# A decoder layer on one core: pieces of TensorE's work parted at their inputs, and softmax sums taken from tiles that GpSimd has added

## What is computed

```python
x = x + self_attention(layernorm(x))              # 16 heads of 16, q and k rotated by position
x = x + cross_attention(layernorm(x), ctx_1024)   # 16 heads of 16, 77 keys
x = x + ffn(layernorm(x))

def ffn(inputs):                                  # six nodes, each an attention of 8 heads of 32
    nodes = {-1: inputs}
    for c in range(6):
        nsrc = min(c + 1, 5); snode = c - nsrc
        q = ew[c, 0] * (nodes[c - 1] @ We[lind + nsrc - 1] + be[...])
        k = ew[c, 1] * (nodes[snode] @ We[lind] + be[...])
        v = ew[c, 2] * (nodes[snode + nsrc // 2] @ We[lind + nsrc // 2] + be[...])
        nodes[c] = act_w[c] * mha(q, k, v, Wq[c], Wk[c], Wv[c], Wo[c]) + q
        lind += nsrc
    return layernorm(nodes[5], ln_g, ln_b)
```

## Time and profile before

| | |
|---|---|
| median of 3 runs | 5605.14 us |
| lowest and highest | 5601.58 and 5607.79 us |
| profiled execution | 5609.61 us, its span 5607.0 us |
| mean granted clock of TensorE | 0.945 of full speed |
| transfers | 46.66 MB, mean 8 GB/s |

### The profile page before, as it was taken

How to read it: one execution, slowest core, us unless ns; L and a number is a source line. 1 busy time by engine, 2 the same in 40 slices (tenths; PEclk the granted TensorE clock), 3 DMA queues, 4 the chain that set the end, 5 groups by cost and what they waited for, 6 DMA issues and landing times.

```text
span 5607.0 us, 154314 instructions
## 1 busy us (share of the span) xinstructions
PE 5142.0 (92%) x64216; PEld 3781.3 (67%) x64216; DVE 2855.0 (51%) x5090; ACT 2527.1 (45%) x4784; POOL 655.8 (12%) x1753
## 2 busy tenths in 40 slices
PE   5898999989999898998989999898998989989899
PEld 5576666767667676676767667676676766667676
DVE  2545554454554545455454554555445455554545
ACT  0354444444445354444444445444444444445444
POOL 0101001010110201001010110201002010110201
PEclk8899998999989899998999989899898999989999
DMA  3000000000000000000000000000000000000000
GB/s 120 6 2 10 3 2 11 2 11 2 7 5 2 11 2 10 3 2 11 2 11 2 6 7 2 11 2 10 3 2 11 2 10 3 6 7 2 11 2 7
DMA packets 45078, 46.66 MB, mean 8 GB/s; under 512 B 11968, under 2 KB 44096, under 8 KB 44352
## 3 DMA queue, kind: packets, MB, share of 16 engines
q1 hardware_dynamic: 36480, 28.59, 1.7%
q10 hardware_dynamic: 7872, 7.76, 0.4%
HBM read 27.95 MB, written 8.39 MB: 6 GB/s over the span
## 4 chain that ended last, share of the span: by engine, by line
issue 82%; POOL 9%; PE 2%; DVE 2%; POOLq 1%; DVEq 0%; ACT 0%; ACTq 0%
POOL neg_max L649 3%; POOL neg_max L652 2%; PE banks L856 2%; POOL x_tok L634 2%; POOL inv_std L628 1%; POOL rope_c L641 1%; DVE n_tok L788 0%; DVE rope_s L801 0%; POOL var_eps L625 0%; POOL node_t L659 0%; POOL node_t L656 0%; POOLq L648 0%; POOLq L651 0%; PE banks L915 0%; DVE rope_s L797 0%
## 5 line engine op out<-in xcount | busy, mean ns | idle before, releaser
L826 DVE TENSOR_REDUCE row_max<-banks 128x4 f32<-128x1024 f32 (+1 forms) x1288 | 1317.6, 1069 | 746.6 <-PE banks L856 711.3
L740 ACT ACTIVATE probs<-banks 128x1024 f32<-128x1024 f32 (+1 forms) x1288 | 1147.3, 936 | 608.0 <-PE banks L856 604.1
L856 PE MATMUL banks<-q_parts,k_parts 32*128 32x256 f32 x12384 | 591.6, 302 | 114.1 <-DVE row_max L826 69.4
L856 PEld LDWEIGHTS banks<-q_parts,k_parts 32*128 32x128 f32 x12384 | 464.3, 192 | 308.9 <-DVE row_max L826 187.4
L856 PE MATMUL banks<-k_parts,q_parts 32*128 32x256 f32 x12432 | 527.5, 302 | 148.2 <-DVE row_max L826 68.6
L837 DVE TENSOR_TENSOR probs<-banks,context_t 128x256 f32<-128x256 f32 x449 | 190.0, 423 | 903.2 <-ACT context_t L752 899.7
L856 PE MATMUL banks<-node_t,w_n 128*128 128x256 f32 x2560 | 641.7, 386 | 0.4
L856 PEld LDWEIGHTS banks<-k_parts,q_parts 32*128 32x128 f32 x12432 | 430.0, 193 | 298.9 <-issue 133.1
L649 POOL TENSOR_TENSOR neg_max<-row_max,zeros 128x8 fp32r<-128x8 f32 x644 | 141.5, 220 | 3749.5 <-DVE row_max L826 3749.5
L856 PEld LDWEIGHTS banks<-node_t,w_n 128*128 128x128 f32 x2560 | 461.9, 190 | 93.8 <-issue 26.3
L750 ACT ACTIVATE context_t<-banks 128x256 f32<-128x256 f32 x514 | 196.6, 383 | 611.6 <-PE banks L856 607.4
(11 more groups left out here) (126 smaller groups left out, 6485.0 us busy)
## 6 DMA issues: line engine op xcount, KB each, us to landing
x_next<-in_x SPq DMA_DIRECT2D x34, 256.0 KB, 2.6
out_y<-x_tok SPq DMA_DIRECT2D x32, 256.0 KB, 2.1
w_head<-in_wf SPq DMA_DIRECT2D x2, 1536.0 KB, 12.8
...
w_n<-in_we ACTq DMA_DIRECT2D x3, 256.0 KB, 11.5
```

The costliest lines, as they stand in the source:

```text
L740: done(act.activation(probs[s][0:rows, g % 2, 2 * p:2 * p + 2, 0:kt, :] .rearrange("p c k t -> p c (k t)"), psum[0:rows, b0:b0 + 2, 0:kt * T],
L826: done(dve.reduce_max(row_max[s][:, g, 2 * p:2 * p + 2, :].rearrange("p c q -> p (c q)"), psum[:, b0:b0 + 2, :].rearrange("p c (q t) -> p ...
L856: return nc.tensor.matmul(bank_ap, lhs, rhs, start=start, stop=stop, **kw)
```

## The change

- **Sums.** A new kind PA on GpSimd adds the probabilities of the two key tiles, one operation for two heads (p = 0 into `n_tok`, p = 1 into a new buffer `pair_sums`). PV keeps only the values; a new kind PS multiplies the added tiles by ones, 4 matmuls in place of 8. In cross attention PS takes the probabilities themselves. EX now waits for PV and PA of the buffer's last user, RC for PS, and LNN of stage 0 also for the last PS, since `n_tok` is shared.
- **Parted pieces.** Q becomes Q and QB (first and second half c of the input), each waiting for its half of the node; QH, QL and NE become one piece for each half d. S becomes S (high by high, high by low) and SB (low by high). ST becomes ST (the scores, waiting for the parts) and SX (the maxima, waiting for MR). OUT becomes OA (the query input) and two OB (one for each half of the context, each waiting for its NR).
- **Buffers.** `kx_parts` goes; cross attention keeps its keys in `k_parts`.
- **Order and banks.** `ORDER` is a new table with 942 words where it had 676. The loop's branch, before between S1.0.1 and S1.0.2, is now between K1.0 and OB0.0.1.

```diff
+            elif k == "PA":
+                g, p = a[3:]
+                both = probs[s][:, g % 2, 2 * p:2 * p + 2, :, :]
+                pool.wait_ge(sem["exp_done"], reached(at, "exp_done", ("EX", s, j, g, p)))
+                pool.wait_ge(sem["sums_ready"], reached(at, "sums_ready", old_sums(s, j, g)))
+                done(pool.tensor_tensor(added(s, p), both[:, :, 0, :], both[:, :, 1, :], ALU.add), "tiles_added", a)
...
+                old = old_probs(s, j, g)
+                act.wait_ge(sem["context_ready"], reached(at, "context_ready", ("PV",) + old))
+                if old[1] == CROSS:
+                    act.wait_ge(sem["sums_ready"], reached(at, "sums_ready", ("PS",) + old))
+                else:
+                    act.wait_ge(sem["tiles_added"], reached(at, "tiles_added", *[("PA",) + old + (i,) for i in range(2)]))
...
-                for what in range(2):
-                    for q in range(kt):
-                        for c in range(4):
-                            if what == 0:
-                                lhs = ones[0:m, :] if j >= FFN0 else half_ones[0:m, 16 * e:16 * e + 32]
...
+                for c in range(4):
+                    lhs = ones[0:m, :] if j >= FFN0 else half_ones[0:m, 16 * e:16 * e + 32]
+                    rhs = probs[s][0:m, g % 2, c, 0, :] if j == CROSS else added(s, c // 2)[:, c % 2, :]
+                    last = matmul(bank_of(a)[ROWS * c:ROWS * (c + 1), T:2 * T], lhs, rhs, False, True,
+                                  skip_group_check=True)
+                done(last, "sums_ready", a)
...
+                q_half = (s, j, 1 if j == SELF else x)
+                if k == "S":
+                    wait_for(pe, at, a, ("high_kept", ("QH",) + q_half), ("low_kept", ("KL", s, j)))
+                else:
+                    wait_for(pe, at, a, ("low_kept", ("QL",) + q_half))
...
-                wait_for(pe, at, a, ("max_rows_kept", ("MR", s, j, x)))
+                wait_for(pe, at, a, ("low_kept", ("QL", s, j, 1 if j == SELF else x)), ("low_kept", ("KL", s, j)))
...
+            elif k == "SX":
+                x, e = place(j, a[3])
+                wait_for(pe, at, a, ("max_rows_kept", ("MR", s, j, x)))
...
+                wait_for(pe, at, a, *(node_kept(s, j, "q") if k == "OA" else [("normalized", ("NR", s, j, a[3]))]))
```

Two lines of the new table, from stage 4:

```diff
+V0.4@5 VE0.4 S0.4.1@0 SB0.4.1 Q1.4@7 QB1.4 QH1.4.0 QH1.4.1 MT0.4.0@6 MR0.4.0 MX0.4.1.1 MX0.4.1.0 NM0.4.1
+ST0.4.0@0 SX0.4.0 EX0.4.0.1 PA0.4.0.1 EX0.4.0.0 PA0.4.0.0 QL1.4.0 QL1.4.1 S1.4.0@4 SB1.4.0 MX1.4.0.0 MX1.4.0.1
```

411 lines of the change are left out of this document (232 added, 179 removed).

## The result

| | before | after |
|---|---|---|
| median | 5605.07 us | 5755.25 us |
| lowest and highest | 5601.58 and 5607.79 us | 5752.68 and 5759.41 us |
| profiled execution | 5609.61 us | 5759.41 us, its span 5757.6 us |
| mean granted clock of TensorE | 0.945 | 0.929 |
| ratio to before | 1 | 1.0269, 95% interval 1.0251 to 1.0287 |

The account below looks back on a forecast made before the run. TensorE, busy 92% of the span, was taken as the bound. Terms of -14.1 + 2.4 + 2.9 + 1 + 1 + 0.6 gave -6.2 us a round, times 16, and -10 once: 5500 us from 5605, range 5400 to 5610.

Parts of the forecast that it names:

- The step that failed: Feed-forward stages: apart from the priced waits, parted pieces and adds were called well covered, so no cost was counted.
- The rival on GpSimd: Self-attention waits for GpSimd's adds at 1.72 us each: +1 us a round, 5611, with the clock below 5630; chance 0.14.
- The sums' matmuls: TensorE's matmuls with ones, 8 fewer in each of 32 groups: 14.1 us a round saved.
- The four waits of 1.2 us: Stages 3 to 6, TensorE waiting for slot 0's probabilities; net +2.4 us a round after old waits are covered.
- The step into stage 2: K0.3, TR1.2 and Q1.2 on TensorE wait for residual, layer norm and copy with less cover: +2.9 us a round.
- The head of slot 1: Branch leaves the maxima, but residual, layer norm, transpose and projection lack cover: +1 us a round, bounds -2 and +5.
- Self-attention of slot 0: GpSimd's eight adds and final scaling against some 16 us of TensorE pieces: +1 us a round, bounds 0 and +4.
- Changes of tile shape: TensorE's matmul shape changes go from 162 to 168 a round at 0.1 us each: +0.6 us a round.
- Ahead of the loop: Pieces before the loop's first scores no longer issued ahead: -10 us, once.
- The clock: Rival: new waits at stage 2 and slot 1's head keep the clock low, 3 us a round lost, 5548; chance 0.13.
- What was said of the profile after: Signs: ones at 3072 instructions, 64 adds a round, TensorE busy 220 us less, its waits 30 to 33 us a round.
- I am wrong if the round is over 336: Refutation sign; bracketed reasons: an add above 1.6 us in self-attention, or slot 1's head longer than taken.

Follow-up runs that it names:

- nm_first: The kernel after the change with three negated maxima moved ahead of the adds they stood behind in GpSimd's queue; 5565.0 us, 0.9926 of before.
- adds_first: The kernel after the change with two adds of slot 1, stage 6 moved ahead of a negated maximum in GpSimd's queue; 5696.8 us, 1.0161 of before.
- no_adds: The kernel after the change without GpSimd's adds: sums take both key tiles by 8 matmuls, parted pieces and order stay; 5600.3 us, 0.9992 of before.
- queue_all: The kernel after the change with the moves of nm_first and adds_first plus two places in self-attention, only GpSimd's order differing; 5481.9 us, 0.9775 of before.

## Why the prediction was wrong, point by point

**The step that failed** is the sentence "Elsewhere in these stages I find the parts well covered: the add has 3.3 us or more against 3.5". It compares the chain exponentials, add, sums with TensorE's pieces between them, and takes each add as if GpSimd had nothing else. I had asked what the add waits for, and not what waits behind the add. The second question has its answer in the table that I had before me: a negated maximum stands behind adds of a later exponential at three places in the feed-forward stages, and adds behind a maximum at one. Price: 16.8 us a round by nm_first and adds_first (12.9 and 3.9), as much as the gap to the forecast (16.7).

**That the rest fits is partly luck.** With the queue in order the round is 331.2 us for 331.8, but its parts are not those of the sum. Against the kernel before, the work is down by 9.5 us where 13.5 was forecast, the waits are up by 4.1 where 7.3 was forecast, and the clock takes 1.4 less, for which the sum has no term. A miss of 4.0 one way and two of 3.2 and 1.4 the other way cancel; the last is within what a round shifts by itself.

**The rival on GpSimd** named the mechanism in half a sentence ("the same queue carries the negated maxima of the next scores") and then priced something else: slower adds, in self-attention, from 1.66 us. The adds took 1.28 us in the mean, as said, and the moves in self-attention gave 0.5 us. The rival came true at another place and by another price, and 0.14 was too low for it: an engine at 45% that gets long operations with waits ahead of short operations on the critical path deserved to be the main rival.

**The sums' matmuls**, 14.1 us: about right. By the split of one round, no_adds has 12.2 us more work than queue_all; by that of the next round 13.6. The rows agree: next to a projection, at the new place, 8 instructions take 0.55 us from start to start in the kernel after and 16 take 0.97 in no_adds, 0.42 for each of 32 groups, 13.4 us. The kernel after, then no_adds:

```profile
1346.68 0.39 PE L930 MATMUL banks<-n_tok,ones 128*32 128x256 f32 x2
...
1347.23 2.00 PE L930 MATMUL banks<-h_t,w_n 128*128 128x256 f32 x8
```
```profile
1306.93 1.05 PE L919 MATMUL banks<-probs,ones 128*32 128x256 f32 x16
1307.90 1.99 PE L919 MATMUL banks<-h_t,w_n 128*128 128x256 f32 x8
```

**The four waits of 1.2 us** before the values of slot 0 in stages 3 to 6 are there: 1.06, 0.88 and 1.40 us, and in stage 6, in queue_all, 0.47 (in the kernel after the negated maxima take its place). 3.8 for 4.8.

```profile
1365.39 1.07 PE L930 MATMUL banks<-probs,v_full 128*32 128x256 f32 x16 [1.06 <-ACT probs L809]
...
1401.66 1.07 PE L930 MATMUL banks<-probs,v_full 128*32 128x256 f32 x16 [0.88 <-ACT probs L809]
...
1440.41 1.07 PE L930 MATMUL banks<-probs,v_full 128*32 128x256 f32 x16 [1.40 <-ACT probs L809]
```

**The step into stage 2**, 2.9 us: K0.3 waits 0.78 and Q1.2 0.69, TR1.2 under 0.15; about 1.5. **The head of slot 1**, +1: the waits from TR1.0 to the scores of cross attention sum to 10.0 us for 8.6, so +1.4. The branch left the maxima, as said, and lies now ahead of the residual; VectorE, then TensorE:

```profile
1581.13 0.69 DVE L919 TENSOR_TENSOR x_tok<-banks,x_tok 128x512 f32<-128x512 f32 x1 [2.95 <-issue]
```
```profile
1585.25 1.12 PE L977 MATMUL banks<-ident,n_tok 128*128 128x128 f32 x4 [3.22 <-DVE n_tok L856]
```

**Self-attention of slot 0**, +1: 6.8 us of waits for 6.1. **Changes of tile shape**, 0.6: the new order's work is 2.7 us above that of before (no_adds, 301.1 for 298.4), so this or something like it was sized too low. In the old order 16 instructions for the sums, ahead of the values with the same tile shape, took 0.88 us; at the new place they take 0.97. That is the term by which the work misses its forecast. **Ahead of the loop**, -10: the same piece of the first round starts at 182.8 for 181.8 us, but from that piece of the last round to the end are 5.3 us for 15.9; together -9.6.

**The clock.** I had asked what 6 us more of low clock would cost, in the attentions. It came where it had never been, behind the waits of over 2 us in the feed-forward part, and cost 8.0 us a round there (212.0 - 19.4 waits - 184.7 work); the attentions lost 3.3 less. Over the round +4.8.

**What was said of the profile after:** ones at 3072 instructions, GpSimd's line at 64 a round and 1.3 us: right. Waits of 30 to 33 us a round: 40.0. TensorE's busy time 220 us lower: 81, since the work fell by 9.6 us a round and not by 13.5, and since instructions at half rate are busy longer (4.8 us a round). "I am wrong if the round is over 336": it is 348.5. The two reasons that stood in brackets behind it were both false.
